# A two-layer graph network on one core: the order of work from the end of the update to the output

## The chip, the cores and the metric

The kernel runs on one core of a Trainium2 chip. The metric is the device time of one execution in microseconds (us). A core has five engines with queues of their own: TensorE (PE in the profile, with its weight loads as PEld), VectorE (DVE), ScalarE (ACT), GpSimd (POOL) and SyncE (SP), which here only issues transfers. They wait for each other through semaphores.

## The reference, cut to what matters

```python
# x [256, 1024]; W [1024, 1024]; a [1, 2048]; 8192 edges
x = layernorm(x + L0(x, src, dst, ...))          # L0: edge attention, then the update
h = x @ W
al, ar = h @ a[0, :1024], h @ a[0, 1024:]
e = exp(-leaky_relu(al[src] + ar[dst], 0.1))
rowsum = segment_sum(e, src)
h_prime = segment_sum(e[:, None] * h[dst], src) / (rowsum[:, None] + 1e-5)
x = layernorm(x + elu(h_prime))
```

L0 ends in the update: `relu([x, z] @ W_hn + b_hn)` for the first 64 rows and `relu([x, z] @ W_on + b_on)` for the other 192, where z is the attention's weighted sum.

## The kernel before, in words

**Tiling.** The 256 nodes are two halves of 128 rows (index h or m), the 1024 features 8 pieces of 128 (KC, index c). Fp32 products that need full precision are made of two rounded parts: every weight matrix is streamed in chunks of 128 rows by 1024, two chunks to a transfer of 1 MB into one of four slots of `W_raw`. `high(n)` (ScalarE, line 461) rounds chunk n into `W_hi`, `low(n)` (VectorE, line 726) subtracts that from the raw chunk into `W_lo`. Both are rings of four (NB); so `high(n)` waits until TensorE has used the chunk four before it (semaphore `chunk_used`). A few chunks (`apart`) have high parts in buffers of their own. For each chunk and half TensorE multiplies `xT_hi` by W_hi and W_lo and `xT_lo` by W_hi, into two halves of 512 columns: six matmuls.

**Order.** Everything is written out by hand: each engine's instructions run in the order of its own function, and named stages (`PE_STAGES`, `ACT_STAGES`, `DVE_STAGES`) count how far an engine is. `link` makes VectorE wait for its own instruction, `stage(name)` lets others wait for it. Chunks 48 to 79 are the update's, 80 to 87 are the second layer's W.

**Update to second layer.** TensorE runs the last four chunks of the update in two passes (`update`, lines 1393 and 1394): first the part that belongs to rows 0 to 127, then rows 128 to 255. Meanwhile ScalarE, after the casts of chunks 76 to 79, loads the table for the square root (`warm_up`, line 652), copies two quarter results from PSUM (lines 655 and 657), and VectorE merges them, adds x and makes the row sums (`merge`, lines 1022 and 1023), then the mean (`mean0`). ScalarE makes the squared deviation (line 634) and the root (line 640), VectorE the inverse (line 1034) and x1 (line 1038). TensorE transposes x1's first half, eight blocks (line 1399); ScalarE rounds it (`x1_high`, line 649), VectorE makes its lows (`x1_low`, line 1043), and TensorE starts h = x1 @ W (`h_chunk`, line 1409): chunks 80 to 83 with half 0, with the eight transposes of half 1 behind the second chunk, chunks 80 to 83 with half 1, chunks 84 to 87 with half 0 (end: stage `h_0`), then chunks 84 to 87 with half 1, first columns 0 to 511 (`h_1`), then the rest. The casts and lows of chunks 78 to 83 lie between these steps.

**Attention.** VectorE takes the two dot products of h's rows with the vector a (`dot`, line 1072: half 0 whole, half 1 in two pieces). The first product, spread on a diagonal (`source_dots`, line 1077), goes through a matmul with ones (stage `al`, then `albc`, line 1431) that gives al to every partition. VectorE adds ar (line 1098), makes the leaky relu (line 1099), ScalarE the exponential (line 675), VectorE multiplies by the number of edges (line 1103, stages `ET0`, `ET1`). ScalarE copies h to SBUF (line 672).

**Output.** TensorE makes half 0 of h_prime with eight instructions (`hp`, line 1435, stage `hp0`), then the row sums (line 1446, `sums`), then half 1. Row sums become inverses (lines 1106 to 1108). ScalarE makes the relu (line 679) and the exponential (line 683) of the elu, VectorE joins them (`elu_and_add`, lines 1115 and 1117). A second layer norm follows: deviations on ScalarE, one half after the other, each with its root; `normalise` on VectorE; half 1's last 512 columns on ScalarE (line 701). Three transfers take the result out: half 0 (line 344), then the two column halves of half 1 (lines 346 and 704). GpSimd subtracts 1 from x1 (line 447), beside it all, once x1 is transposed.

Of the kernel before, what the change touches and what calls it, by code (L numbers as in the profile page):

```python
# [5 lines left out]
P = 128  # L6
N = 256
# [32 lines left out]
def gnn_two_layers(nc, x, src, dst, W_hh, b_hh, W_oo, b_oo, W_ho, b_ho, W_a, b_a, W_hn, b_hn, W_on, b_on,  # L40
# [6 lines left out]
    with ctx:  # L47
# [50 lines left out]
        y_sums, less_mean, squares, rstd = (small[:, k:k + 4] for k in (46, 50, 54, 58))  # L98

# [140 lines left out]
        x1_less_one = sem("x1_less_one")  # L240
        squared = sem("squared")
# [42 lines left out]
        def halves(n):  # L284

            if apart(n):
                return hi_apart[n - END["hoB"] - NB], lo_in_raw[:, n // 2 % NS, n % 2, :]
            return W_hi[:, ring(n), :], W_lo[:, ring(n), :]

        def lo_count(n, pool):  # L290
# [5 lines left out]
                     "x1T0", "x1T1", "h_0", "h_1", "albc", "hp0", "sums", "hp1", "hp2"]  # L296
        ACT_STAGES = ["xT0", "xT1", "hh_x", "ooB_out", "C_hh", "C_oo", "L_oo", "L_hh", "counts", "parts", "soft0", "soft1", "zT0", "both0", "zT1",
                      "both1", "q0_low", "q1_low", "sd0", "x1T0", "sd1", "x1T1", "h1_0", "h1_1",
                      "exp0", "exp1", "h_relu0", "h_exp0", "h_exp1", "h_relu1", "h_exp2", "h_relu2", "sd2", "sd3", "out3"]
        DVE_STAGES = ["xT0", "xT1", "tot", "totals", "columns", "ooA_out", "placed0", "placed1", "keys", "key_u8", "hoA_b",  # L300
                      "hoA_lo", "hoB_lo", "maxima", "P", "PT", "parts", "zT0",
                      "zT1", "mean0", "x1_0", "mean1", "x1T0", "x1_1", "x1T1", "dots0", "al", "dots1", "lr0", "lr1", "ET0", "ET1",
                      "row_sums", "mean2", "mean3", "out0", "scale3", "out1"]
# [14 lines left out]
        def _(sp):  # L318
# [27 lines left out]
            sp.dma_start(out[P:N, 0:512], y2[:, 1, 0:512]).then_inc(out_in, 16)  # L346
# [4 lines left out]
        def _(pool):  # L351
# [93 lines left out]
            ga.nop().then_inc(pick_made, 1)  # L445
            pool.wait_ge(pe_step, pe_at("x1T1"))
# [4 lines left out]
        def _(act):  # L451
# [178 lines left out]
            highs(UX + 4, END["hn"])  # L630
# [16 lines left out]
            def x1_high(h):  # L647
                act.wait_ge(pe_step, pe_at(f"x1T{h}"))
                sa.copy(xT_hi[:, :, h * P:(h + 1) * P], G0[:, h * D:(h + 1) * D].rearrange("p (c n) -> p c n", n=P)) \
                    .then_inc(act_step, 1)  # L650

            warm_up(ACT.Sqrt, 0)

# [821 lines left out]
```

## Time and profile before

| | us |
|---|---|
| median of 3 runs | 364.58 (363.96 to 365.58) |
| the profiled execution, its own time | 364.0 |
| its span, first to last instruction | 361.9 |
| PE, DVE, ACT, POOL busy in the span | 323.3, 292.6, 195.6, 109.2 |
| mean granted TensorE clock in the span | 0.959 of full speed |

The span is what the trace covers; 2.1 us of the execution's own time lie around it. The rows come from a timeline (instructions in order of time), from groups of instructions, and from windows, which give busy times and the granted clock of a stretch. Where an engine was idle before an instruction, brackets give that time and who ended it. A matmul's printed duration overlaps the next one's.

### The profile page before, as it was taken

To read this page: it belongs to the slowest core of one execution; us is meant where nothing else is said; L and a number is where in the kernel's file an instruction comes from. 1 tells how busy PE (TensorE), PEld (TensorE's weight loads), DVE (VectorE), ACT (ScalarE), POOL (GpSimd) and SP (SyncE) were. 2 spreads that over 40 slices of the span, in tenths; PEclk is the share of its full clock that TensorE was granted. 3 is DMA by queue.
4 is the path that set the end of the run, shared out by engine and by line. 5 is a ranking of instruction groups with operands and counts; after the bars stand their busy time and mean duration, and the time that the engine had idled before them with its cause. 6 is when DMAs were issued, how large, how long until landed. Compare 5 with 4: busy or idle time off the path is not lost.

```text
span 361.9 us, 4632 instructions
## 1 busy us (share of the span) xinstructions
PE 323.3 (89%) x1440; PEld 250.2 (69%) x1440; DVE 292.6 (81%) x418; ACT 195.6 (54%) x300; POOL 109.2 (30%) x123
## 2 busy tenths in 40 slices
PE   2889999999999997999999999995899997799480
PEld 1768887677645785788888888783687875588230
DVE  0799999967699978799999999986958678745535
ACT  3754396203044236788888887454435677353255
POOL 4300061083001900188889888300000000050000
PEclk9999999999999999899999999998899999699796
DMA  6999499789999994003030000026635984000003
GB/s 229 404 406 361 173 308 388 235 279 239 325 321 309 390 366 192 2 0 118 3 116 2 1 3 0 2 63 227 232 117 201 358 283 203 0 2 1 0 0 116
DMA packets 17638, 63.10 MB, mean 174 GB/s; under 512 B 2234, under 2 KB 2236, under 8 KB 17360
## 3 DMA queue, kind: packets, MB, share of 16 engines
q1 hardware_dynamic: 13520, 50.07, 37.8%
q0 software_dynamic: 2096, 8.74, 8.3%
q10 hardware_dynamic: 2000, 4.00, 3.4%
q8 instruction: 13, 0.21, 0.2%
q14 instruction: 9, 0.07, 0.1%
HBM read 59.64 MB, written 3.16 MB: 174 GB/s over the span
## 4 chain that ended last, share of the span: by engine, by line
PE 68%; DVE 21%; ACT 5%; issue 3%; DMA 2%; SPq 0%; DVEq 0%; ACTq 0%
PE ps L1313 21%; PE ps L1160 12%; PE ps L1204 8%; PE ps L1409 7%; DVE W_lo L731 5%; PE ps L1347 5%; PE ps L1320 3%; PE ps L1355 3%; PE ps L1179 3%; DMA x_nat<-in_x_dram 2%; PE ps L1435 2%; ACT W_hi L466 1%; DVE tile_val L751 1%; PE ps L1236 1%; PE ps L1218 1%
## 5 line engine op out<-in xcount | busy, mean ns | idle before, releaser
L466 ACT CAST W_hi<-W_raw 128x1024 fp32r<-128x1024 f32 x68 | 69.3, 1046 | 62.4 <-DMA W_raw<-in_L_gnn_W_ho_dram 24.6
L731 DVE TENSOR_TENSOR W_lo<-W_raw,W_hi 128x1024 fp32r<-128x1024 f32 x64 | 76.5, 1223 | 16.6 <-ACT W_hi L466 13.8
L968 DVE SCALAR_TENSOR_TENSOR ps<-ps,wa_bc 128x1024 f32<-128x1024 f32 x74 | 87.6, 1256 | 2.8 <-PE ps L1313 2.7
L1313 PE MATMUL ps<-A_tab,oh 128*128 x148 | 53.9, 446 | 2.4 <-ACT oh L575 2.4
L1160 PE MATMUL ps<-W_hi,xT_hi 128*128 128x512 f32 x112 | 46.4, 414 | 0.7 <-DVE W_lo L731 0.7
L1313 PE MATMUL ps<-B_tab,oh 128*128 x148 | 47.0, 399 | 0.0
L1160 PE MATMUL ps<-W_lo,xT_hi 128*128 128x512 f32 x112 | 44.2, 394 | 0.0
L1160 PE MATMUL ps<-W_hi,xT_lo 128*128 128x512 f32 x112 | 34.9, 393 | 0.0
L422 POOL TENSOR_SCALAR sc<-sc 128x256 f32<-128x256 f32 x37 | 32.7, 883 | 3.3
L420 POOL TENSOR_TENSOR sc<-irow,keys 128x256 f32<-128x256 f32 x37 | 23.8, 642 | 32.4 <-PE ps L1320 32.1
L581 ACT ACTIVATE sc<-sc,keys 128x64 f32<-128x64 f32 x74 | 24.4, 341 | 16.2 <-DVE ps L968 16.1
L1313 PEld LDWEIGHTS ps<-B_tab,oh 128*128 128x128 f32 x148 | 28.4, 192 | 5.4
L1320 PEld LDWEIGHTS ps<-sc 128*128 128x128 f32 x148 | 27.3, 189 | 6.4 <-issue 0.2
L447 POOL TENSOR_SCALAR x<-x 128x2048 f32<-128x2048 f32 x1 | 5.4, 5390 | 83.8 <-PE ps L1399 83.8
L1204 PE MATMUL ps<-W_raw,hh_x 128*128 128x512 f32 x64 | 28.2, 593 | 0.0
L1313 PEld LDWEIGHTS ps<-A_tab,oh 128*128 128x128 f32 x148 | 24.3, 192 | 3.9 <-issue 3.3
L1160 PEld LDWEIGHTS ps<-W_hi,xT_hi 128*128 128x128 f32 x112 | 21.5, 192 | 6.8 <-DVE W_lo L731 1.9
L568 ACT ACTIVATE oh_dist<-key_rows,pcol 128x512 bf16<-128x512 uint8 x37 | 26.1, 706 | 0.0
L575 ACT ACTIVATE oh<-oh_dist 128x512 fp32r<-128x512 bf16 x37 | 23.2, 626 | 3.6 <-PE ps L1313 3.2
L1160 PEld LDWEIGHTS ps<-W_lo,xT_hi 128*128 128x128 f32 x112 | 21.3, 191 | 4.7 <-issue 0.7
L1160 PEld LDWEIGHTS ps<-W_hi,xT_lo 128*128 128x128 f32 x112 | 21.3, 190 | 4.7
L1320 PE MATMUL ps<-sc 128*128 128x64 f32 x148 | 24.1, 247 | 0.0
(255 smaller groups left out, 553.4 us busy)
## 6 DMA issues: line engine op xcount, KB each, us to landing
W_raw<-in_L_gnn_W_oo_dram SPq DMA_DIRECT2D x8, 1024.0 KB, 9.7
W_raw<-in_L_gnn_W_ho_dram SPq DMA_DIRECT2D x8, 1024.0 KB, 5.2
W_raw<-in_L_gnn_W_hh_dram SPq DMA_DIRECT2D x8, 1024.0 KB, 8.6
W_raw<-in_L_gnn_W_hn_dram SPq DMA_DIRECT2D x8, 1024.0 KB, 5.2
W_raw<-in_L_gnn_W_on_dram SPq DMA_DIRECT2D x8, 1024.0 KB, 4.9
W_raw<-in_L_gnn_W_dram SPq DMA_DIRECT2D x4, 1024.0 KB, 4.9
key_rows<-key_rows_scratch POOLq DMA_DIRECT2D x1, 2304.0 KB, 13.9
table_scratch<-tabs ACTq DMA_DIRECT2D x2, 1024.0 KB, 6.4
```

The costliest lines, as they stand in the source:

```text
L420: link(ga.tensor_tensor(pair, irow[:, 1:Q + 1].unsqueeze(1).unsqueeze(1).broadcast_to([P, 2, 2, Q]), keys[:, t:t + 2, 0:2].unsqueeze(3).br ...
L422: ga.tensor_scalar(pair, pair, 0.0, None, ALU.is_equal).then_inc(ends_made, 1)
L466: sa.copy(halves(n)[0], W_raw[:, n // 2 % NS, n % 2, :]).then_inc(hi_made, 1)
L568: sa.activation(oh_dist[:, j % 2, :, :], key_rows[:, :, 2 * j * P:2 * (j + 1) * P], ACT.Abs, bias=pcol[:, 1:2]).then_inc(dist_made, 1)
L581: sa.activation(sc[:, t % U, 2, :], sc[:, t % U, 1, :], ACT.Copy, scale=keys[:, t, 2:3]) \
L731: v.tensor_tensor(lo, W_raw[:, n // 2 % NS, n % 2, :], hi.bitcast(F32), ALU.subtract).then_inc(lo_made, 1)
L968: v.scalar_tensor_tensor(acc, acc, 0.0, wa_bc[:], ALU.max, ALU.mult, accum_out=keys[:, t, 2:3]).then_inc(reduced, 1)
L1160: ins = mm(acc[:, m * D + f:m * D + f + 512], x_part(n - first, m), W[:, f:f + 512], start=(n == first and x_part is hi and W is W1), stop ...
L1204: ins = mm(G0[:, f:f + 512], hh_x[:, row // KC, row % KC, :], W_raw[:, n // 2 % NS, n % 2, f:f + 512], start=(row == 0), stop=(row == 2 * ...
L1313: ins = mm(acc[:, n * 512:(n + 1) * 512], oh[:, t // 2 % 2, k, t % 2 * P:(t % 2 + 1) * P], tab[:].rearrange("p q d -> p (q d)")[:, n * 512 ...
L1320: ins = mm(G0[:, bass.ds(column.with_bounds(min_val=0, max_val=15 * Q), Q)], sc[:, t % U, 1:3, :].rearrange("p r n -> p (r n)"), sc[:, t % ...
L1409: ins = mm(G1[:, m * D + f:m * D + f + 512], part[:, c, m * P:(m + 1) * P], W[:, f:f + 512], start=(c == 0 and part is xT_hi and W is W1), ...
```

## The change

It acts on seven places, all but one behind the last casts of the update:

1. Chunks 80 and 81 get high parts in two separate buffers, and are cast by ScalarE and subtracted by VectorE before the square root's table load and the merges. The casts of the six other chunks stand one place or more earlier in the row as well. The lows of all eight overwrite the raw chunk.
2. x1's first half is normalised, transposed, rounded and given its lows in two pieces of four blocks.
3. TensorE runs chunks 80 to 85 (not 83) with half 0 and then half 1; behind these are left two chunks (not four) with half 0 (`h_0`) and with half 1.
4. GpSimd negates the second half of a (`bias_bc[:, 1, :]`, 128 by 1024) once the last biases are there; VectorE's dots then give -ar.
5. exp(-leaky_relu(s)) becomes the smaller of exp(-s) and exp(-0.1 s): ScalarE makes both from PSUM, VectorE takes the minimum and multiplies. The adding and the leaky relu on VectorE go.
6. TensorE makes the row sums of each half ahead of that half's part of h_prime; ScalarE makes the exponential ahead of the relu.
7. In the last layer norm half 0's squared deviation goes from ScalarE to VectorE, behind `mean3`; one root and one inverse serve both halves; VectorE normalises half 1 whole; half 1 goes out as two transfers of 64 rows.

```diff
+            return END["hoB"] + NB <= n < UX or END["upd"] <= n < END["upd"] + 2
...
+            if late(n):
+                return (hi_apart[2 + n - END["upd"]] if apart(n) else W_hi[:, ring(n), :]), in_place
...
-            sp.dma_start(out[P:N, 0:512], y2[:, 1, 0:512]).then_inc(out_in, 16)
+            sp.dma_start(out[P:P + Q, :], y2[0:Q, 1, :]).then_inc(out_in, 16)
...
+            pool.wait_ge(biases_in, 112)
+            ga.tensor_scalar(bias_bc[:, 1, :], bias_bc[:, 1, :], -1.0, None, ALU.mult).then_inc(less_target, 1)
...
-            highs(UX + 4, END["hn"])
+            highs(UX + 4, END["upd"] + 2 - NB)
...
             warm_up(ACT.Sqrt, 0)
             act.wait_ge(chunk_used, END["hn"])
             sa.copy(y2[0:Q, 0, :], G0[Q:P, D:2 * D]).then_inc(act_step, 1)
             act.wait_ge(pe_step, pe_at("q1"))
             sa.copy(y2[Q:P, 0, :], G1[0:Q, 0:D]).then_inc(act_step, 1)
-            highs(END["hn"], END["hn"] + 2)
+            high(END["upd"] + 2)
+            high(END["upd"] + 3)
             act.wait_ge(dve_step, dve_at("mean0"))
             deviation(0, x1[:, 0, :])
-            root(0, 1)
-            highs(END["hn"] + 2, END["upd"])
-            x1_high(0)
+            root(0, 1, 1)
+            high(END["upd"] + 4)
+            x1_high(0, 0, KC // 2, "x1T0a")
             act.wait_ge(dve_step, dve_at("mean1"))
             deviation(1, x1[:, 1, :])
-            root(1, 2)
-            x1_high(1)
-            highs(END["upd"], END["h1"])
+            root(1, 2, 2)
+            high(END["upd"] + 5)
+            x1_high(0, KC // 2, KC, "x1T0b")
+            x1_high(1, 0, KC, "x1T1")
+            high(END["upd"] + 6)
+            high(END["upd"] + 7)
...
+            def powers(h):
+                sa.activation(PT[:, h, :], G0[:, 0:N], ACT.Exp, bias=dots[:, h, 1:2], scale=-1.0)
+                sa.activation(y2[:, 1, h * N:(h + 1) * N], G0[:, 0:N], ACT.Exp, bias=slopes[:, h:h + 1], scale=-SLOPE) \
+                    .then_inc(act_step, 1)
...
+            act.wait_ge(dve_step, dve_at("dots0"))
+            h_copy(0, 0, D)
+            act.wait_ge(dve_step, dve_at("dots1a"))
+            h_copy(1, 0, 512)
+            act.wait_ge(pe_step, pe_at("albc"))
+            powers(0)
+            act.wait_ge(dve_step, dve_at("dots1"))
+            powers(1)
+            h_copy(1, 512, D)
...
-            act.wait_ge(dve_step, dve_at("mean2"))
-            deviation(0, h1[:, 0, :])
-            root(0, 3)
+            warm_up(ACT.Sqrt, 0)
             act.wait_ge(dve_step, dve_at("mean3"))
             deviation(1, h1[:, 1, :])
-            root(1, 4)
+            act.wait_ge(dve_step, dve_at("square2"))
+            root(0, 2, 3)
...
-            lows(UX + NB + 4, END["upd"])
+            lows(UX + NB + 4, END["upd"] + 2)
...
-            low(END["upd"])
-            inverse(0, "sd0")
-            normalise(x1[:, 0, :], y1[:, 0, :], 0)
-            stage("x1_0")
+            low(END["upd"] + 2)
+            inverse(0, 1, "sd0")
+            normalise(x1[:, 0, 0:512], y1[:, 0, 0:512], 0)
+            stage("x1_0a")
...
-            low(END["upd"] + 1)
-            x1_low(0)
-            inverse(1, "sd1")
+            x1_low(0, 0, KC // 2, "x1T0a")
+            low(END["upd"] + 3)
+            normalise(x1[:, 0, 512:D], y1[:, 0, 512:D], 0)
+            stage("x1_0b")
+            inverse(1, 2, "sd1")
             normalise(x1[:, 1, :], y1[:, 1, :], 1)
             stage("x1_1")
-            lows(END["upd"] + 2, END["upd"] + NB)
-            x1_low(1)
-            lows(END["upd"] + NB, END["h1"])
+            low(END["upd"] + 4)
+            x1_low(0, KC // 2, KC, "x1T0b")
+            low(END["upd"] + 5)
+            x1_low(1, 0, KC, "x1T1")
+            lows(END["upd"] + 6, END["h1"])
...
+            link(v.tensor_scalar(slopes[:, 0:1], dots[:, 0, 1:2], SLOPE, None, ALU.mult))
             stage("dots0")
...
-                link(v.tensor_scalar(PT[:, h, :], G0[:, 0:N], dots[:, h, 1:2], None, ALU.add))
-                link(v.scalar_tensor_tensor(PT[:, h, :], PT[:, h, :], SLOPE, PT[:, h, :], ALU.mult, ALU.max))
...
+                link(v.tensor_tensor(PT[:, h, :], PT[:, h, :], y2[:, 1, h * N:(h + 1) * N], ALU.min))
                 link(v.tensor_tensor(PT[:, h, :], PT[:, h, :], S_cnt[:, 0, h, :], ALU.mult))
...
-            inverse(0, "sd2")
+            link(v.scalar_tensor_tensor(h1[:, 0, :], y1[:, 0, :], less_mean[:, 0:1], y1[:, 0, :], ALU.add, ALU.mult,
+                                        accum_out=squares[:, 0:1]))
+            stage("square2")
+            inverse(0, 2, "sd2")
             normalise(y2[:, 0, :], y1[:, 0, :], 0)
             stage("out0")
...
-            normalise(y2[:, 1, 0:512], y1[:, 1, 0:512], 1)
+            normalise(y2[:, 1, :], y1[:, 1, :], 1)
...
+            both = END["upd"] + 6
+            transpose_x1(0, 0, KC // 2, "x1_0a", "x1T0a")
+            pe.wait_ge(dve_step, dve_at("x1T0a"))
+            for n in range(END["upd"], both):
+                if n == END["upd"] + KC // 2:
+                    pe.wait_ge(dve_step, dve_at("x1T0b"))
                 h_chunk(n, 0, (0, 512))
...
                 pe.wait_ge(dve_step, dve_at(f"ET{hd}"))
+                for hs in range(2):
+                    ins = mm(bank(1 + hs)[:, 0:1], PT[:, hd, hs * P:(hs + 1) * P], ones_f[:, 0:1],
+                             start=(hd == 0), stop=(hd == 1))
+                if hd == 1:
+                    stage(ins, "sums")
```

## Rows read from the trace of the kernel before

**Rows 1.** The page's chain that ended last, shares of the span by engine:

```profile
PE 68%; DVE 21%; ACT 5%; issue 3%; DMA 2%; SPq 0%; DVEq 0%; ACTq 0%
```

**Rows 2.** Timeline, end of update to restart: start us, us, engine line op [idle before <-releaser]:

```profile
293.89 2.95 ACT L466 CAST W_hi<-W_raw 128x1024 fp32r<-128x1024 f32 x3 [1.29 <-PE ps L1355]
296.85 1.28 ACT L645 ACT_TABLE_LOAD   x1
298.36 1.01 ACT L655 COPY y<-ps 64x1024 f32<-64x1024 f32 x1
...
304.72 1.15 ACT L634 ACTIVATE x<-y,small 128x1024 f32<-128x1024 f32 x1 [0.77 <-DVEq L724]
...
307.45 1.48 PE L1399 MATMUL ps<-ident,x 128*128 128x128 f32 x8 [2.12 <-DVEq L724]
...
311.52 0.79 PE L1409 MATMUL ps<-W_hi,xT_hi 128*128 128x512 f32 x1 [2.59 <-DVEq L724]
```

**Rows 3.** Timeline, the attention's dots and h_prime:

```profile
331.11 1.23 DVE L1072 SCALAR_TENSOR_TENSOR y<-ps,bias_bc 128x1024 f32<-128x1024 f32 x1 [3.50 <-PE ps L1409]
...
336.20 0.69 DVE L1072 SCALAR_TENSOR_TENSOR y<-ps,bias_bc 128x512 f32<-128x512 f32 x1 [0.69 <-PE ps L1409]
...
337.52 0.70 PE L1431 MATMUL ps<-y,ones_f 128*128 128x256 f32 x2 [1.44 <-DVEq L724]
...
341.31 5.79 PE L1435 MATMUL ps<-h,PT 128*128 128x512 f32 x8 [3.09 <-DVEq L724]
```

**Rows 4.** Timeline, row sums and the exponential behind them:

```profile
346.94 0.95 PE L1446 MATMUL ps<-ones_f,PT 128*128 128x1 f32 x8
...
348.38 1.11 ACT L683 ACTIVATE y<-ps,small 128x1024 f32<-128x1024 f32 x1 [0.21 <-DVEq L724]
```

**Rows 5.** Timeline, the last layer norm:

```profile
355.97 1.15 ACT L634 ACTIVATE h<-y,small 128x1024 f32<-128x1024 f32 x1 [0.59 <-DVEq L724]
...
358.92 0.34 ACTq L704 DMA_DIRECT2D out_dram<-y  x1
```

**Rows 6.** Windows: PE, PEld, DVE, ACT, POOL busy us, PEclk, DMA share, GB/s:

```profile
314.50:315.00 0.50, 0.50 (x3) 0.36 (x3) 0.50 (x1) 0.00 (x0) 0.00 (x0) 0.66 0.00 0
...
338.50:339.00 0.50, 0.00 (x0) 0.00 (x0) 0.41 (x1) 0.46 (x1) 0.00 (x0) 0.73 0.00 0
...
345.50:346.00 0.50, 0.50 (x2) 0.19 (x1) 0.00 (x0) 0.00 (x0) 0.00 (x0) 0.94 0.00 0
```

**Rows 7.** Timelines of POOL and its neighbours on DVE and ACT, four stretches:

```profile
118.61 0.60 POOL L435 CAST x_both<-xT_hi 128x512 fp32r<-128x512 f32 x1
118.88 0.35 DVE L867 TENSOR_TENSOR rest<-st_logit,part_f 128x1 f32<-128x1 f32 x1
...
239.53 1.91 ACT L612 CAST bn_parts<-y 64x2048 fp32r<-64x2048 f32 x1 [1.60 <-DMA y<-in_L_gnn_b_on_dram]
241.69 0.70 DVE L901 TENSOR_TENSOR S_log<-S_log,junk 128x512 f32<-128x512 f32 x1
...
317.03 5.39 POOL L447 TENSOR_SCALAR x<-x 128x2048 f32<-128x2048 f32 x1 [83.83 <-PE ps L1399]
318.03 1.23 DVE L1043 TENSOR_TENSOR xT_lo<-ps,xT_hi 128x1024 fp32r<-128x1024 f32 x1 [2.96 <-ACT xT_hi L649]
...
322.28 1.23 DVE L731 TENSOR_TENSOR W_lo<-W_raw,W_hi 128x1024 fp32r<-128x1024 f32 x1 [3.02 <-ACT W_hi L466]
```

**Rows 8.** Groups kept apart by shape, 295 to 362 us: xcount | busy us, mean ns:

```profile
L1038 DVE TENSOR_SCALAR x<-y,small 128x1024 f32<-128x1024 f32 x2 | 1.6, 813 | 0.1
...
L1103 DVE TENSOR_TENSOR PT<-PT,S_cnt 128x256 f32<-128x256 f32 x2 | 0.8, 425 | 0.3
...
L675 ACT ACTIVATE PT<-PT 128x256 f32<-128x256 f32 x2 | 0.8, 418 | 0.8 <-DVEq L724 0.7
...
L1038 DVE TENSOR_SCALAR y<-y,small 128x512 f32<-128x512 f32 x1 | 0.5, 546 | 0.1
```

**Rows 9.** Transfers, 355 to 362 us in 40 slices: GB/s moved:

```profile
GB/s 0 0 0 0 0 0 0 0 0 0 0 0 0 0 0 0 23 468 398 398 374 445 398 421 71 0 211 374 398 386 375 375 374 386 117 0 0 0 0 0
```

More of the change, by code:

```diff
@@ L635, in deviation, with root @@
                     .then_inc(squared, 1)
-            def root(h, nth):
+            def root(a, b, nth):
                 act.wait_ge(squared, nth)
-                sa.activation(deviations[:, h:h + 1], squares[:, h:h + 1], ACT.Sqrt, bias=eps_ln[:, 0:1], scale=1.0 / D) \
+                sa.activation(deviations[:, a:b], squares[:, a:b], ACT.Sqrt, bias=eps_ln[:, 0:1], scale=1.0 / D) \
                     .then_inc(act_step, 1)
@@ L1087, in _ @@
                 dot(1, k, 0, 512, dot_parts[:, 0, k:k + 1])
+            stage("dots1a")
             dve.wait_ge(chunk_used, END["h1"])
@@ L1094, in _ @@
                     stage("al")
+            link(v.tensor_scalar(slopes[:, 1:2], dots[:, 1, 1:2], SLOPE, None, ALU.mult))
             stage("dots1")
-            dve.wait_ge(pe_step, pe_at("albc"))
-            for h in range(2):
-                link(v.tensor_scalar(PT[:, h, :], G0[:, 0:N], dots[:, h, 1:2], None, ALU.add))
-                link(v.scalar_tensor_tensor(PT[:, h, :], PT[:, h, :], SLOPE, PT[:, h, :], ALU.mult, ALU.max))
-                stage(f"lr{h}")
             for h in range(2):
                 dve.wait_ge(act_step, act_at(f"exp{h}"))
+                link(v.tensor_tensor(PT[:, h, :], PT[:, h, :], y2[:, 1, h * N:(h + 1) * N], ALU.min))
                 link(v.tensor_tensor(PT[:, h, :], PT[:, h, :], S_cnt[:, 0, h, :], ALU.mult))
@@ L1394, in _, with transpose_x1 @@
             update(END["hn"], END["upd"], (1,))
-            def transpose_x1(h):
-                pe.wait_ge(dve_step, dve_at(f"x1_{h}"))
-                for c in range(KC):
+            def transpose_x1(h, a, b, ready, name):
+                pe.wait_ge(dve_step, dve_at(ready))
+                for c in range(a, b):
                     ins = nc.tensor.transpose(G0[:, h * D + c * P:h * D + (c + 1) * P], x1[:, h, c * P:(c + 1) * P],
                                               ident[:])
-                stage(ins, f"x1T{h}")
+                stage(ins, name)
             def h_chunk(n, m, columns):
@@ L1439, in _ @@
                 pe.wait_ge(dve_step, dve_at(f"ET{hd}"))
-                pe.wait_ge(act_step, act_at("h1_1"))
+                for hs in range(2):
[3 more added lines that the diff above has]
+                    stage(ins, "sums")
                 for n in range(2):
+                    if hd and n:
+                        pe.wait_ge(act_step, act_at("h1_1"))
                     ins = hp(0, n, hd)
             stage(ins, "hp0")
-            for hs in range(2):
-                for hd in range(2):
-                    ins = mm(G0[:, 512 + hs * N:512 + hs * N + 1], PT[:, hd, hs * P:(hs + 1) * P], ones_f[:, 0:1],
-                             start=(hd == 0), stop=(hd == 1))
-            stage(ins, "sums")
             for n in range(2):
```

82 lines of the change are left out of this document (38 added, 44 removed).

## The prediction

> **What bounds the kernel now.** I read the page's chain first: it lies 68% on PE and 21% on DVE [rows 1], so an edit pays where PE stands still or where the chain has left it. All of the change but one instruction acts on the last 65 us; there the timeline shows where PE stops. Behind the update it waits until 311.52, with eight transposes between at 307.45 [rows 2]; behind h it stops at about 336.1 and starts h_prime at 341.31 [rows 3]; from the row sums on, the chain is ACT and DVE alone, until the last transfer is issued at 358.92 [rows 4, 5]. The windows show a second cost of these stops: the granted clock is 1.2 GHz (0.50) when PE restarts, and is back at 2.4 GHz at about 314.8 and 345.5, 3.3 and 4.2 us after the restarts [rows 3, 6]. The groups by shape give durations.
>
> **1. GpSimd's scaling of a: +0.65.** The new instruction is not free, though POOL stands idle for 83.8 us [rows 7]. It may start when the last bias lands, at 239.5 (ACT's cast starts there). It is half as large as the 5.39 us subtraction of the same kind [rows 7]: some 2.8 us with its fixed part, so it ends at about 242.3. On DVE, L901 is due at 241.69, a TENSOR_TENSOR with both inputs in SBUF, in the unbroken chain of the softmax. Can it run beside POOL? At 118.88 a TENSOR_TENSOR with both inputs in SBUF, of one column, ran from 118.88 to 119.23, and POOL's cast from 118.61 to 119.21: an operation so small that lasts until POOL's is over has waited for it. Against this, a subtraction at 322.28 began 0.14 us before POOL's end at 322.42 and took its usual 1.23 [rows 7]; but an end that is off by 0.14 explains that. I take the wait: 242.3 - 241.7 = 0.65, ends 0 and 0.7. DVE's chain carries it to the zT stage, where PE waits.
> The Trainium skill's page "SBUF — State Buffer", section "Who interferes with whom", says that a VectorE instruction with two SBUF inputs and a GpSimd instruction that reads SBUF exclude each other, and the one issued second waits for the whole of the first. By that rule the sum holds the 0.65; by the row of 322.28 alone it would be 0.65 less. The row of 118.88 agrees with the rule.
>
> **2. From the update to PE's restart: -0.2.** ACT's last three casts end at 296.85, the table load follows at once, then L655 at 298.36 [rows 2]. That copy's data have been there since PE finished chunk 75; ACT alone makes it late. Two more casts ahead of the table load, at a third of 2.95 us each [rows 2], push L655 and all behind it (second copy, two merges, mean0) by 1.9. The squared deviation then starts at 306.6, not 304.72. What comes back: the casts of 82 and 83 fill ACT's wait for mean0. On DVE, one subtraction (1.2 us) leaves the path between x1 and its lows; the half normalisation takes 0.55 instead of 0.81 [rows 8]; four transposes instead of eight save half of 1.48 [rows 2], though DVE's sum of y1's second half (1.3 us) hides that; the half lows take 0.69 instead of 1.23, the price of 512 columns from PSUM [rows 3]. Step by step: x1's first piece is there at 309.0, four transposes end at 309.85, the half cast at 310.45, the half lows at 311.2, PE starts at 311.3. So 1.9 lost, 2.1 won. The second piece, chunk 84's lows and half 1's lows all come before PE needs them: x1T0b by 317.6 against 319.8, x1T1 by 320.8 against 322.5, chunk 86's lows by 329.0 against 330.8. PE's matmuls for h are the same number and have no new stop.
>
> **3. The dots: +2.05.** Before, 24 matmuls lie between h_0 and h's end, and DVE's dots start at 331.11 and 336.20 [rows 3]: 5.09 us. After, 12 lie between, so 2.55. DVE now needs 5.65 us from the first dot to `al` (331.11 to 337.45, just ahead of the broadcast at 337.52, less 0.69 idle; [rows 3]) and 0.2 more for the slope's multiply. Before, PE's end covered all but 1.25 of it. After: 336.20 - 2.55 + 5.85 = 339.5, against 337.45. DVE becomes the bound here, and the last pieces of h are ready first. Ends: 1.85 to 2.2.
>
> **4. Two exponentials: -0.95.** From `al` to the first matmul of h_prime it was 337.45 to 341.31, 3.86 us [rows 3]. After: the broadcast, 0.70 before [rows 3], which now comes at 339.5, behind the clock's fall at about 338.7 [rows 6], so at 1.2 GHz about 0.95 with its start; two exponentials of 0.42 [rows 8] behind it; minimum and product, 0.425 each [rows 8]; 0.3 for six handovers. Sum 2.9. The exponential's source in PSUM and the copies of h in between cost nothing: ACT has finished them by 338.6.
>
> **5. Row sums ahead, exponential ahead of relu: +0.35 and -1.25.** Before, hp0 takes 5.80 (341.31 to 347.11), and the exponential starts 1.27 later, behind relu, sums and inverse [rows 4]. After, it starts at once: -1.25, because the sums end 1.7 us before hp0. But PE makes them first: eight instructions took 0.80 at 2.4 GHz [rows 4]; four at 1.2 GHz cost 0.8 to 1.3, four at 2.4 GHz 0.4, and of the former half comes back, as less of h_prime then runs at 1.2 GHz. Together 0.6 with a restart as slow as before, 0.2 with one of 3.4 us; I take 0.35. The relu is behind the exponential but ends before DVE's first addition does.
>
> **6. The last layer norm: +1.0.** Before, mean3 releases the deviation at 355.97, and the last transfer is issued at 358.92, 2.95 us later [rows 5]. After: square on DVE 1.3 (beside ACT's), root 0.3, inverse 0.2, normalise half 0 0.81, half 1 0.81 [rows 8], handovers 0.2: 3.6. And half 0 goes out only 0.85 before half 1, not 1.8. In the slices of 0.175 us the two halves of the output moved at about 390 GB/s, with a pause between [rows 9]. After, 1 MB moves in one stretch of 2.65 us that begins some 0.85 behind the first issue (358.75 in this execution's times), and ends at 362.2 against 361.2. So +1.0, +0.65 if only the issue counts.
>
> **Sum.** 0.65 - 0.2 + 2.05 - 0.95 + 0.35 - 1.25 + 1.0 = +1.65. Some 0.1 of step 2 and 0.1 to 0.2 of step 5 depend on when the clock rises; I round to +1.5. The profiled execution took 364.0 (span 361.9), so 365.5; the median of the runs, 364.58, is 0.6 above it, so 366.1. A measurement of this kernel can't tell less than 0.5% (1.8 us) from no change; the forecast is just within it, and the ends of the steps (0 in step 1, 1.85 and 2.2 in step 3, 0.2 and 0.6 in step 5, 0.65 in step 6) give 364.8 to 367.1.
>
> **Rivals.**
> *POOL's scaling is hidden* (12%): step 1 is 0, as by the row of 322.28; 364.58 + 0.9 = 365.5.
> *The clock isn't lowered in a gap* (10%): in the gap ahead of h, PE ran 1.48 us of transposes and still restarted at 1.2 GHz [rows 2, 6]; the new gap has fewer. Against it, then; but the new broadcast at 339.5 lies in the middle of the second gap. A restart at 2.4 GHz gives back half of 3.3 to 4.2 us: about 364.2, and 362.4 if both gaps keep the clock. This one ends faster.
> *DVE's lows behind POOL* (6%), slower: POOL's subtraction of 5.39 us starts when half 1's transposes end, 318.45; DVE's `low(85)`, with both inputs in SBUF, is due at 317.6. Should it come second, it waits until 323.9, half 1's lows come at 326.4 instead of 320.8, and PE, free at 322.5, waits 3.9 us: 370.0. It decides when DVE is more than 0.85 us later than drawn. The lows themselves, one input in PSUM, do run beside POOL: 1.23 at 318.03 [rows 7].
> *A slower restart* (10%), slower: the dots leave PE idle for 3.4 us before the broadcast and 1.7 behind it. If the clock stays at 1.2 GHz through the first half of h_prime, step 5 costs 2 more: 368.
> *The change doesn't do what it says*: x1 by pieces is meant to bring PE's restart forward, and the two early casts take all of that back. That is in the forecast, as step 2.
>
> **How the numbers follow.** Forecast 62%, the rivals 12, 10, 6 and 10%. Slower by over 0.5% means above 366.4: about two fifths of the forecast's case, and both slow rivals: 0.42. Faster by over 0.5% (below 362.8) needs the clock in both gaps: 0.06. The rest, 0.52, is within. The range goes from the one gap with a clock kept to the slower restart: 364.0 to 368.0; it leaves out the double clock case and the wait behind POOL.
>
> **What would show it.** Step 1: L901's place (the TENSOR_TENSOR behind the reciprocal) takes 1.3 instead of 0.70. Step 2: the first copy of the quarters starts 1.9 later behind the last cast of chunk 79, PE's restart lies within 0.3 of 6.2 us behind the update's end. Step 3: no idle time on DVE between the dots, `al` 3.4 us behind PE's last matmul of h instead of 1.3. Step 4: 2.9 us from there to h_prime. Step 5: row sums long ready, an exponential at once behind hp0. Step 6: 3.6 us from mean3 to the last issue, one stretch of transfers. Wrong would be: DVE idle between the dots, a stop of PE among h's matmuls, or a restart at the full clock.

## The result, and the profile of the changed kernel

The changed kernel takes 370.13 us (median of 4 runs, 369.62 to 371.23), the kernel before 364.73 beside it: a ratio of 1.0166, 95% interval 1.0136 to 1.0196. A second series, below, gave 369.16 and a ratio of 1.0127 (1.0098 to 1.0156). The forecast was 366.1, 1.5 us above the kernel before, with a range from 364.0 to 368.0: the direction was right, the size less than a third of the true one (5.4 us, and 5.0 in the second series). The runs of the kernel before fall in two groups, and its one trace is of the second: of 17 runs beside experiments 1 to 4, 7 took 362.9 to 363.3 at a mean granted clock of 0.963, and 10 took 364.1 to 365.5 at 0.959.

| | before | changed, first trace | changed, second trace | forecast |
|---|---|---|---|---|
| update's end | 305.33 | 307.90 | 305.61 | +0.65 |
| from there to h's first matmul | 6.19 | 6.30 | 6.30 | -0.2 |
| h | 24.56 | 25.37 | 25.48 | 0 |
| h's end to the broadcast of al | 1.44 | 3.46 | 3.46 | +2.05 |
| to h_prime's first instruction | 3.79 | 3.13 | 3.13 | -0.95 |
| to the elu's exponential | 7.07 | 7.71 | 7.73 | -0.9 |
| to the last deviation | 7.59 | 7.59 | 7.59 | 0 |
| to the last transfer's issue | 2.95 | 3.85 | 3.84 | +0.65 |
| to the span's end | 2.96 | 4.18 | 4.19 | +0.35 |
| span | 361.88 | 369.49 | 367.33 | +1.65 |

The table is worked out from starts and ends in the timelines (us); the line for the update's end is a time in the span, the others are lengths. The columns before and second trace differ by 5.45 in all: 0.28 + 0.11 + 0.92 + 2.02 - 0.66 + 0.66 + 0.89 + 1.23. The first trace holds 2.3 us more ahead of the update's end than the second. The 0.28 at the update's end is not shown to be the change's: in the traces of experiments 2 to 6 and 9 to 11, which differ by one instruction at most up to there, the update's end lies between 304.15 and 306.27.

The timeline of the changed kernel (first trace) around the update's end, 307.90:

```profile
299.30 1.99 ACT L477 CAST hi<-W_raw 128x1024 fp32r<-128x1024 f32 x2
301.31 1.28 ACT L655 ACT_TABLE_LOAD   x1
302.82 1.01 ACT L664 COPY y<-ps 64x1024 f32<-64x1024 f32 x1
...
311.63 1.12 PE L1426 MATMUL ps<-ident,x 128*128 128x128 f32 x4 [3.72 <-DVEq L747]
...
314.20 0.80 PE L1436 MATMUL ps<-hi,xT_hi 128*128 128x512 f32 x1 [1.46 <-DVEq L747]
```

The two early casts stand ahead of the table load. Against [rows 2] the transposes have shrunk from 1.48 to 1.12 and the second wait of PE from 2.59 to 1.46, but the first has grown from 2.12 to 3.72.

From the dots to the exponential, the same trace:

```profile
341.70 0.69 DVE L1100 SCALAR_TENSOR_TENSOR y<-ps,bias_bc 128x512 f32<-128x512 f32 x1
...
343.03 1.22 PE L1463 MATMUL ps<-y,ones_f 128*128 128x256 f32 x2 [3.46 <-DVEq L747]
...
346.16 1.01 PE L1473 MATMUL ps<-ones_f,PT 128*128 128x1 f32 x4 [1.91 <-DVEq L747]
347.03 3.76 PE L1467 MATMUL ps<-h,PT 128*128 128x512 f32 x4
...
353.87 1.11 ACT L710 ACTIVATE y<-ps,small 128x1024 f32<-128x1024 f32 x1 [7.54 <-PE ps L1467]
```

The third pair of dots carries no bracket: DVE no longer waits for PE, as it did by 0.69 in [rows 3], and PE waits 3.46 for the broadcast's operand. The granted clock of that stretch (windows; columns as in [rows 6]):

```profile
345.00:348.00 3.00, 1.84 (x5) 1.35 (x6) 1.70 (x4) 1.34 (x4) 0.00 (x0) 0.50 0.00 0
348.00:351.00 3.00, 3.00 (x7) 1.42 (x5) 0.00 (x0) 0.00 (x0) 0.00 (x0) 0.50 0.00 0
351.00:354.00 3.00, 3.00 (x8) 1.63 (x8) 0.32 (x2) 0.13 (x1) 0.00 (x0) 0.76 0.00 0
```

0.76 of the last 3 us is a rise at about 352.4, 6.3 us behind h_prime's start; in the kernel before it came 4.2 us behind [rows 3, 6].

The end, timeline and transfer issues (KB each, us from issue to landing):

```profile
361.46 1.15 ACT L645 ACTIVATE h<-y,small 128x1024 f32<-128x1024 f32 x1 [1.47 <-DVEq L747]
361.53 1.28 DVE L1154 SCALAR_TENSOR_TENSOR h<-y,small 128x1024 f32<-128x1024 f32 x1 [0.16 <-DVE small L1051]
...
365.31 0.55 ACTq L727 DMA_DIRECT2D out_dram<-y  x1
```

```profile
out_dram<-y SPq DMA_DIRECT2D x1, 512.0 KB, 2.6
out_dram<-y SPq DMA_DIRECT2D x1, 256.0 KB, 3.1
out_dram<-y ACTq DMA_DIRECT2D x1, 256.0 KB, 3.8
```

In the kernel before, the last transfer was issued 2.95 us behind the deviation [rows 5], here 3.85; and the last landing takes 3.8 us.

### The profile page after: what moved, and what is told of

It is laid out like the page before. It is cut to its first block, busy times and chain, and to the rows that moved or that the text cites. A ratio compares the mean times of both kernels' runs of the same rounds, so it can differ in the third digit from the quotient of the medians.

```text
span 369.5 us, 4635 instructions
## 1 busy us (share of the span) xinstructions
PE 327.0 (88%) x1440; PEld 252.6 (68%) x1440; DVE 293.6 (79%) x420; ACT 194.5 (53%) x301; POOL 110.9 (30%) x124
## 4 chain that ended last, share of the span: by engine, by line
PE 69%; DVE 20%; ACT 5%; issue 2%; DMA 2%; SPq 0%; DVEq 0%; ACTq 0%
PE ps L1340 21%; PE ps L1187 11%; PE ps L1231 7%; PE ps L1436 6%; DVE W_lo L754 5%; PE ps L1374 5%; PE ps L1347 3%; PE ps L1382 3%; PE ps L1206 3%; PE ps L1467 3%; DMA x_nat<-in_x_dram 2%; PE ps L1406 1%; ACT W_hi L477 1%; DVE tile_val L774 1%; DVE y L1100 1%
## 5 line engine op out<-in xcount | busy, mean ns | idle before, releaser
L477 ACT CAST W_hi<-W_raw 128x1024 fp32r<-128x1024 f32 x66 | 67.2, 1045 | 65.0 <-DMA W_raw<-in_L_gnn_W_ho_dram 24.7
L754 DVE TENSOR_TENSOR W_lo<-W_raw,W_hi 128x1024 fp32r<-128x1024 f32 x56 | 66.8, 1222 | 13.3 <-ACT W_hi L477 11.2
```

The source lines that it names most:

```text
L477: sa.copy(halves(n)[0], W_raw[:, n // 2 % NS, n % 2, :]).then_inc(hi_made, 1)
L754: v.tensor_tensor(lo, W_raw[:, n // 2 % NS, n % 2, :], hi.bitcast(F32), ALU.subtract).then_inc(lo_made, 1)
```

## The experiments

Each was run beside the kernel before on the same chip, whose medians were 364.11 to 364.19. A difference "by the ratios" is the difference of two ratios to the kernel before, times 364. The theory at first: my steps hold, and what is missing in the sum is time at 1.2 GHz. The rival: work that I did not count.

### 1. and 2. Both kernels with PE kept busy in its gaps

```diff
+            def fill(b, count):
+                for _ in range(count):
+                    mm(bank(b), zT_hi[:, 0, 0:P], flat(zT_hi, 0, 2), start=True, stop=True, skip_group_check=True)
...
+            fill(0, 8)                       # changed kernel: 14
             transpose_x1(0)
+            fill(3, 10)                      # changed kernel: 6
             pe.wait_ge(dve_step, dve_at("x1T0"))
...
+            fill(3, 5)                       # changed kernel: 13
             pe.wait_ge(dve_step, dve_at("al"))
             stage(mm(G0[:, 0:N], ones_f[:], y2[:, 0, 0:N], start=True, stop=True), "albc")
+            fill(3, 12)                      # changed kernel: 9
```

> The kernel before with 35 matmuls whose results nobody reads, on PE where it stands idle: 8 ahead of x1's first transposes, 10 behind them, 5 ahead of the broadcast of al, 12 behind it, each some 0.23 us at 2.4 GHz. Clock theory: PE restarts at the full clock in both places, which gives back half of the 3.3 us before h's clock rises and half of the 4.2 us in h_prime, so 1.5 to 3.7 us less than before. Rival (the clock costs nothing, other engines set the end): within 0.5 us of before.

Measured: 360.29 us, ratio 0.9901 (0.9882 to 0.9920): 3.9 us faster, just past the expected 3.7. The clock stays at 2.4 GHz from the update to h_prime's end.

> The changed kernel with 42 such matmuls in its own gaps: 14 ahead of the first transposes, 6 behind, 13 ahead of the broadcast, 9 behind. Clock theory: what the change lost beyond the 1.5 us of my sum (5.4 measured) is longer time at 1.2 GHz (10.2 us at a stretch in h_prime's trace instead of 6.8, and later in h), so this kernel is 3 to 5 us faster than the changed one, and 1 to 2 us slower than the kernel before with such matmuls. Rival (work I did not count on ACT, DVE or in transfers): it stays 4 us or more behind the kernel before with such matmuls.

Measured: 363.92 us, ratio 1.0004 (0.9986 to 1.0022), so by the ratios 4.5 us faster than the changed kernel's second series and 5.9 faster than its first. But it is 3.6 us slower than the kernel before with such matmuls, where I expected 1 to 2. Both theories are half right. At the same full clock the two timelines differ as follows: h 23.49 against 22.99; h's end to broadcast 3.46 against 1.44; to h_prime 2.63 against 3.80; to the exponential 4.60 against 4.97; to the last issue (from the last deviation) 3.85 against 2.95; from there to the end 4.19 against 2.96. What the sum did not count is in three places: 0.5 in h, 0.5 of the 0.9 promised by step 5, and 1.1 in the last layer norm and transfers (2.1 against the forecast's 1.0). The way from h_prime's start to the exponential, in this trace:

```profile
341.36 0.58 PE L1481 MATMUL ps<-ones_f,PT 128*128 128x1 f32 x4
341.80 1.96 PE L1475 MATMUL ps<-h,PT 128*128 128x512 f32 x4
...
345.96 1.11 ACT L710 ACTIVATE y<-ps,small 128x1024 f32<-128x1024 f32 x1 [4.45 <-PE ps L1475]
```

### 3. Four chunks left behind h's first part

```diff
-            both = END["upd"] + 6
+            both = END["upd"] + 4
```

> The changed kernel, with chunks 80 to 83 (not 85) through both halves first, so four chunks are left behind them as before: only step 3 undone. My theory: the dots start 2.55 us earlier against h's end, DVE is not the bound, al comes 2.05 us earlier, and h_prime starts that much earlier: 2 us less than the changed kernel, up to 3.5 if the clock has not fallen so far. Rival (the order of chunks is free, the dots lie elsewhere hidden): within 0.5 us of the changed kernel.

Measured: 366.66 us, ratio 1.0067 (1.0043 to 1.0091): 2.2 us less by the ratios against the second series of the changed kernel, 3.6 against the first. VectorE waits again, and h's end to broadcast is 1.36:

```profile
338.72 0.69 DVE L1100 SCALAR_TENSOR_TENSOR y<-ps,bias_bc 128x512 f32<-128x512 f32 x1 [0.77 <-PE ps L1436]
```

Step 3 stands: its row returns with one edit. But that the total came out as expected is partly luck, as two more terms stand in this trace, of opposite sign. PE stops in h, because four chunks with half 0 end ahead of half 1's lows, which are done at 321.92:

```profile
322.03 0.50 PE L1436 MATMUL ps<-hi,xT_hi 128*128 128x512 f32 x1 [1.05 <-DVEq L747]
```

so h takes 26.73 us against 25.48: the two chunks more of step 3 do buy something, which my sum put at nothing. And the clock is back sooner in h_prime, which starts at 342.66:

```profile
343.00:343.50 0.50, 0.50 (x4) 0.40 (x4) 0.47 (x2) 0.00 (x0) 0.00 (x0) 0.96 0.00 0
343.50:344.00 0.50, 0.50 (x2) 0.19 (x1) 0.08 (x1) 0.00 (x0) 0.00 (x0) 0.50 0.00 0
...
346.00:346.50 0.50, 0.50 (x3) 0.13 (x1) 0.00 (x0) 0.00 (x0) 0.00 (x0) 0.50 0.00 0
346.50:347.00 0.50, 0.50 (x6) 0.50 (x4) 0.00 (x0) 0.00 (x0) 0.00 (x0) 0.62 0.00 0
```

The stretch at 1.2 GHz lasts 3.4 us here, against 6.8 in the kernel before and 10.2 in the changed one, and ends 4.2 us behind h_prime's start. From the broadcast to h_prime it is 2.61 instead of 3.13, and from there to the exponential 6.32 instead of 7.73. Against experiment 9 the rows are +1.25, -2.10, -0.52 and -1.41.

### 4. The old layer norm and transfers

The edit puts back the two deviations with a root each on ScalarE, `scale3`, and the transfers by columns, as the kernel before has them.

```diff
-            warm_up(ACT.Sqrt, 0)
+            act.wait_ge(dve_step, dve_at("mean2"))
+            deviation(0, h1[:, 0, :])
+            root(0, 1, 3)
             act.wait_ge(dve_step, dve_at("mean3"))
             deviation(1, h1[:, 1, :])
-            act.wait_ge(dve_step, dve_at("square2"))
-            root(0, 2, 3)
+            root(1, 2, 4)
...
-            link(v.scalar_tensor_tensor(h1[:, 0, :], y1[:, 0, :], less_mean[:, 0:1], y1[:, 0, :], ALU.add, ALU.mult,
-                                        accum_out=squares[:, 0:1]))
...
```

> The changed kernel with the last layer norm and the three transfers of the kernel before: only step 6 undone. My theory: from mean3 to the last issue 2.95 us again instead of 3.85, and the transfers apart again: 1 to 2 us less than the changed kernel. Rival (the transfers end at the same time anyway, as their rate bounds them): less than 0.5 us less.

Measured: 366.89 us, ratio 1.0091 (1.0065 to 1.0117). From the last deviation to the span's end it is 5.90 us, as before (5.91), against 8.03 in the changed kernel. So the part costs 2.1, not 1.0. In time it is 1.3 us less than the second series of the changed kernel by the ratios, 2.3 by the medians; with runs from 365.06 to 367.95 the time alone would not tell, and the trace does.

### 5. Row sums behind, relu first

```diff
-                for hs in range(2):
-                    ins = mm(bank(1 + hs)[:, 0:1], PT[:, hd, hs * P:(hs + 1) * P], ones_f[:, 0:1], ...)
...
             stage(ins, "hp0")
+            for hs in range(2):
+                for hd in range(2):
+                    ins = mm(bank(1 + hs)[:, 0:1], PT[:, hd, hs * P:(hs + 1) * P], ones_f[:, 0:1], ...)
+            stage(ins, "sums")
```

> The changed kernel with the row sums made behind hp0 and the relu ahead of the exponential, as before: only step 6's neighbour, step 5, undone. By my sum this costs 1.25 and returns 0.35: 0.9 us slower than the changed kernel. Clock theory: in the changed kernel's trace h_prime began with four of the one-column matmuls at 346.16 and the clock rose only at 352.4, 6.2 us later, against 4.2 in the kernel before; if the small matmuls at the head delay the rise, this kernel's clock is back up to 3.4 us sooner, which gives back up to 1.7: between 0.8 faster and 0.9 slower than the changed kernel, and from the first hp matmul to hp0's end 5.8 us again. From al to h_prime nothing changes.

Measured: 369.26 us, ratio 1.0125 (1.0089 to 1.0162), the same as the changed kernel within the noise. The timeline:

```profile
343.61 6.58 PE L1467 MATMUL ps<-h,PT 128*128 128x512 f32 x8 [1.91 <-DVEq L747]
350.03 0.95 PE L1479 MATMUL ps<-ones_f,PT 128*128 128x1 f32 x8
```

The eight instructions take 6.5 us instead of the 5.80 of [rows 3, 4], without a small matmul at their head, and the clock is back at 349.5, 5.8 us behind the start (0.55 in the window 349.0 to 349.5, 1.00 in the next). So my idea that the small matmuls delay the clock falls. The way from h_prime's start to the exponential is 7.86 here and 7.73 with the sums ahead: at this clock step 5 by itself is worth 0.13.

### 6. Without GpSimd's scaling

```diff
-            ga.tensor_scalar(bias_bc[:, 1, :], bias_bc[:, 1, :], -1.0, None, ALU.mult).then_inc(less_target, 1)
+            ga.nop().then_inc(less_target, 1)
```

> The changed kernel without GpSimd's scaling of a's second half: it leaves out the negation, so the exponentials get al minus instead of plus the bias; all else is the same work. My step 1 said the scaling costs 0.65 by making a subtraction on VectorE wait. The changed kernel's trace already speaks against it: VectorE's L924 began at 243.05 and took 0.69 while POOL ran from 240.98 to 243.77. So by step 1: 0.65 less than the changed kernel; by that trace: within 0.3.

Measured: 368.90 us, ratio 1.0119 (1.0075 to 1.0163); the changed kernel's second series had 1.0127. From the first copy of the logits on DVE to the zT lows it is 23.81 us with the scaling (trace of experiment 5) and without it. The rows of the changed kernel (first trace) show why:

```profile
240.98 2.79 POOL L456 TENSOR_SCALAR bias_bc<-bias_bc 128x1024 f32<-128x1024 f32 x1 [6.44 <-DMA y<-in_L_gnn_b_on_dram]
```

```profile
243.05 0.69 DVE L924 TENSOR_TENSOR S_log<-S_log,junk 128x512 f32<-128x512 f32 x1
```

The subtraction (VectorE's TENSOR_TENSOR) starts 0.72 us ahead of POOL's end, as far as the trace places that end, and takes its usual time. Step 1 was nothing.

### 7. The casts of 80 and 81 late

```diff
-            highs(UX + 4, END["upd"] + 2 - NB)
+            highs(UX + 4, END["upd"] - NB)
...
             sa.copy(y2[Q:P, 0, :], G1[0:Q, 0:D]).then_inc(act_step, 1)
+            high(END["upd"])
+            high(END["upd"] + 1)
             high(END["upd"] + 2)
```

with VectorE's `low(80)` to `low(84)` one place or more later, between x1's steps. The edit also moves GpSimd's subtraction from x1 behind the last lows, so the two are tested together.

> The changed kernel with the casts and lows of chunks 80 and 81 behind the quarter copies and merges (ScalarE casts 80 to 83 there, VectorE's lows are spread between x1's steps), and GpSimd's subtraction from x1 behind the last lows. Theory of step 2: the first quarter copy starts 1.5 us behind chunk 79's cast again instead of 3.4, mean0 comes 1.9 earlier, and PE's restart some 2 us earlier than in the changed kernel against the update's end (4.2 instead of 6.3). The end follows by 2, give or take 1.7 for the clock. Rival (the early casts are needed, PE then waits for the lows of 80 to 83): PE stops between h's first chunks and less than 0.7 us comes out.

Measured: 366.98 us, ratio 1.0083 (1.0054 to 1.0112): 1.6 us less than the second series by the ratios, 3.0 than the first.

```profile
297.49 1.28 ACT L656 ACT_TABLE_LOAD   x1
299.00 1.01 ACT L665 COPY y<-ps 64x1024 f32<-64x1024 f32 x1
```

```profile
307.82 0.65 PE L1431 MATMUL ps<-ident,x 128*128 128x128 f32 x4 [1.83 <-DVEq L750]
310.22 0.74 PE L1441 MATMUL ps<-hi,xT_hi 128*128 128x512 f32 x1 [1.75 <-DVEq L750]
```

PE restarts 4.23 us behind the update's end (305.99), against 6.30 with early casts and 6.19 before; GpSimd's subtraction starts only at 329.71, far behind it. Step 2's bookkeeping is shown: the pieces win 2 us at the restart, the early casts lose as much.

### 8. What should be kept, with filled gaps

The changed kernel with the edits of 3, 4 and 7, the lows of 84 and 85 behind half 1's, and unread matmuls in the four gaps:

```diff
+            fill(0, 7)
             transpose_x1(0, 0, KC // 2, "x1_0a", "x1T0a")
+            fill(3, 7)
...
+            fill(3, 5)
             pe.wait_ge(dve_step, dve_at("al"))
             stage(mm(G0[:, 0:N], ones_f[:], y2[:, 0, 0:N], start=True, stop=True), "albc")
+            fill(3, 8)
```

> What the steps say should be kept: of the change the two pieces of x1, the lows in place, the two exponentials and the row sums ahead; casts of 80 and 81 late, four chunks left behind h's first part, the last layer norm of before, and 27 unread matmuls that keep PE busy in its gaps. By the steps, against the kernel before with such matmuls (360.29): restart -1.5 (2 won, 0.45 for the four transposes moved behind it), exponentials -1.1, row sums and order -0.4: 357.3, some 7 us less than before. Rival (the pieces only pay where PE is bound, and the lows now come too late at the full clock): 359 to 360.

Measured: 358.64 us, ratio 0.9869 (0.9831 to 0.9907; four runs took 358.28 to 358.64, two 360.86 and 360.89): 1.3 us above the expectation, but the fastest median of this study, 5.5 us below the kernel before (4.8 by the ratio). The timeline of PE shows a wait of 1.04 in h, which is most of the missing part:

```profile
316.12 0.61 PE L1447 MATMUL ps<-W_hi,xT_lo 128*128 128x512 f32 x2
317.79 0.50 PE L1447 MATMUL ps<-hi,xT_hi 128*128 128x512 f32 x1 [1.04 <-DVEq L754]
```

h's first four chunks are done before half 1's lows, as in experiment 3. Against experiment 1 PE restarts 1.94 us earlier (4.23 against 6.17), but h takes 1.82 longer (24.81 against 22.99): of the win of x1's pieces 0.1 is left at the full clock, much as the rival says. What is left of the gain on experiment 1 is 1.2 ahead of h_prime and 0.33 behind its start.

### 9. The changed kernel again

> The changed kernel once more, unchanged. Its first trace had two stretches at 1.2 GHz in code that the change does not touch (3.4 us more at 148, and 263.7 to 267.1 in the second z product), which put the update's end at 307.9, while the traces of four variants have it at 304.2 to 306.0. Theory: that was this execution, not the change; the update ends at 305.3 to 306.3 here and the median lies 5 us above the kernel before, of which 4.65 is the sum of the steps as the variants' traces show them. Rival: the change itself moves that stretch; then the update ends at 307 to 308 again.

Measured: 369.16 us, ratio 1.0127 (1.0098 to 1.0156). The update ends at 305.61. The 2.3 us that the first trace had ahead of it belong to that execution. The other rows agree with the first trace within 0.11 us.

### 10. The last transfers by columns

```diff
-            sp.dma_start(out[P:P + Q, :], y2[0:Q, 1, :]).then_inc(out_in, 16)
+            sp.dma_start(out[P:N, 0:512], y2[:, 1, 0:512]).then_inc(out_in, 16)
...
-            act.dma_start(out[P + Q:N, :], y2[Q:P, 1, :]).then_inc(out_in, 16)
+            act.dma_start(out[P:N, 512:D], y2[:, 1, 512:D]).then_inc(out_in, 16)
```

> The changed kernel with half 1 going out as two transfers of 128 rows by 512 columns (as before) instead of 64 rows by 1024; the last layer norm stays changed. In the changed kernel's trace these took 3.1 and 3.8 us from issue to landing, and 2.0 and 2.6 in the kernel before; from the last issue to the span's end it was 4.2 against 3.0. Theory A (the form of 64 rows): 2.0 to 2.9 again and 0.8 to 1.2 us less at the end. Theory B (they stand behind half 0's 512 KB, issued 1 us before): 3 us or more still, and less than 0.4 us less.

Measured: 368.33 us, ratio 1.0116 (1.0081 to 1.0150); that it is faster than the changed kernel is inside the intervals, so the trace has to tell. Its issues:

```profile
out_dram<-y SPq DMA_DIRECT2D x1, 512.0 KB, 2.7
out_dram<-y SPq DMA_DIRECT2D x1, 256.0 KB, 2.8
out_dram<-y ACTq DMA_DIRECT2D x1, 256.0 KB, 3.1
```

From the last issue to the end it is 3.46 us, against 4.19 with rows and 2.96 before. Of the 1.2 us, 0.7 are the form of 64 rows (theory A). The other 0.5 go with the new layer norm (with the old one, experiment 4, it is 2.95); that they are spent behind half 0's transfer (theory B) fits, but was not tried by itself.

### 11. Only the gap ahead of h_prime filled

The edit of experiment 2 without its first two fills; against that kernel:

```diff
-            fill(0, 14)
...
-            fill(3, 6)
```

> The changed kernel with unread matmuls only in the second gap, 13 ahead of the broadcast of al and 9 behind it. Clock theory: from h_prime's first instruction to the elu's exponential it is 4.6 us (as in the kernel with both gaps filled) instead of 7.6; the broadcast takes 0.70 instead of 1.22; all of 3.4 us is won on the changed kernel, against 1.4 for this gap in the kernel before, where the clock rose 4.2 us behind h_prime's start and not 6. Rival (row sums ahead make the stretch long by themselves): over 5.5 us.

Measured: 365.58 us, ratio 1.0028 (1.0010 to 1.0045): 3.6 us less than experiment 9 in the same series.

```profile
340.78 0.70 PE L1470 MATMUL ps<-y,ones_f 128*128 128x256 f32 x2 [0.46 <-DVEq L747]
...
343.40 0.59 PE L1481 MATMUL ps<-ones_f,PT 128*128 128x1 f32 x4
...
345.66 0.50 PE L1481 MATMUL ps<-ones_f,PT 128*128 128x1 f32 x4
```

```profile
348.02 1.11 ACT L710 ACTIVATE y<-ps,small 128x1024 f32<-128x1024 f32 x1 [4.46 <-PE ps L1475]
```

From h_prime's start to the exponential 4.62 us, against 7.73: in the changed kernel 3.1 us of this stage are the clock. In the kernel before it is 7.07 - 4.97 = 2.1 (experiment 1). That 1.0 is the change's own loss to the clock here.

### 12. Five chunks first, and a gap in the softmax filled

Experiment 8 with one chunk more ahead of half 1, 15 unread matmuls ahead of P's transposes, and one unread matmul more in two of the four gaps; against experiment 8:

```diff
+            low(END["upd"] + 4)
             x1_low(1, 0, KC, "x1T1")
-            lows(END["upd"] + 4, END["h1"])
+            lows(END["upd"] + 5, END["h1"])
...
+            pe.wait_ge(dve_step, dve_at("maxima"))
+            for _ in range(15):
+                mm(bank(1), xT_hi[:, 0, 0:P], flat(xT_hi, 0, 2), start=True, stop=True, skip_group_check=True)
...
-            both = END["upd"] + 4
+            both = END["upd"] + 5
```

> The kernel with late casts, old layer norm and filled gaps (358.64), now with five chunks through both halves first, and the lows of chunk 84 ahead of half 1's, because there PE stopped for 1.2 us (316.6 to 317.8) waiting for half 1's lows; also 15 unread matmuls ahead of the transposes of P. The stop goes but for 0.3, al comes 0.4 later against h's end, the transposes run at 2.4 GHz (0.4): 357.4 to 358. Rival (the stop is taken over by the lows of 84 and 85): 358.6 as before.

Measured: 360.59 us, ratio 0.9887 (0.9850 to 0.9923): slower than expected by 3. The stretch at 1.2 GHz that lay at 250.6 to 257.4 in experiment 8 has moved to 260.4 to 267.3, and now covers the second z product: the update ends at 307.65, not 305.39. The only edit ahead of that place is the 15 unread matmuls, but the first trace of the changed kernel and that of experiment 10 have part of this stretch there without them, so one trace does not settle the cause; one of the six runs took 357.24. Behind the update's end, h is 24.15 instead of 24.81, but h's end to broadcast is 2.10 instead of 1.37: five chunks win nothing on four.

## Why the forecast was wrong

The stages of the two kernels differ by 5.45 in all in the traces; the forecast's sum was 1.65, rounded to 1.5. The step that failed most is step 5: it took 0.9 off where the traces add 0.66, because it let the clock come back in h_prime as soon as before. Beside it, the matmuls of h were put at nothing (0.92) and the last transfers too low (1.23 instead of 0.35). Point by point:

**Step 1 (+0.65) was wrong: 0.** VectorE's subtraction ran beside POOL's scaling (experiment 6). The row of 322.28 in [rows 7], which I explained away with an inexact end, was the one to go by. The wait at 118.88 was real in its row, but it does not carry over to this pair of instructions; what the two cases differ in was not tried. The trace of the kernel before does show the two engines excluding each other elsewhere: GpSimd's TENSOR_SCALAR of line 422 at 119.89 took 1.97 us beside a low of VectorE that began at 119.85 and took 1.23, against 0.88 on average. It may be that GpSimd's work is over some time before its printed end; that is not shown. The rule of the Trainium skill's page "SBUF — State Buffer", section "Who interferes with whom", makes the second instruction wait for the whole of the first; here it did not.

**Step 2 (-0.2): +0.1 at the restart, and 0.5 forgotten.** The two opposed terms are shown by experiment 7 (2.1 us between early and late casts). The forecast's -0.2 against +0.11: the four transposes ran at 1.2 GHz and took 1.12, not 0.75 (0.65 in experiment 7, at 2.4 GHz), which is as much as the miss. The sentence that failed is "PE's matmuls for h are the same number": four of half 0's transposes have moved behind the restart, and PE makes them among h's matmuls. They cost 0.5 (h at full clock 23.49 against 22.99). The rest of the 0.92 in h is the clock, back 4.3 us behind the restart in the second trace instead of 3.3: one microsecond more at half speed.

**Step 3 (+2.05): right for its row, 2.02.** Undone alone it comes back (experiment 3). What the step left out is that the longer gap goes with a later clock, below, and that the two chunks cover a stop of 1.05 us in h.

**Step 4 (-0.95): right in kind, -0.66.** With the clock up it is -1.17 (2.63 against 3.80). At 1.2 GHz the broadcast takes 1.22 instead of 0.70; I had put 0.95 for it.

**Step 5 (-0.9): the wrong sign, +0.66.** It has two errors. The sums' eight instructions all lie ahead of hp0's end now, and hp0 with them takes as much longer as they last, 0.8 at full clock (0.44 and 0.36 between the starts in experiment 2); with them the whole step is -0.37 (4.60 against 4.97). I had allowed 0.35 for them and let a half come back. And I took the clock's return as 3.4 to 4.2 us behind h_prime's start; it came 5.8 to 6.4 us behind it in seven traces (the changed kernel twice, experiments 4 to 7 and 10). That costs the 1.0 of experiment 11. In these seven h_prime starts 6.6 us behind h's end, and the stretch at 1.2 GHz lasts 10.2; in the kernel before it starts 5.2 behind, and the stretch lasts 6.8; in experiment 3, with step 5 in place and four chunks left, 4.0 and 3.4. So it isn't step 5's edit that brings the slow restart; it goes when step 3 alone is undone, and with it the longer gap. The rival "a slower restart" described this, with the dots' gap as its ground, and priced it at 2; it was given 10%.

**Step 6 (+1.0): right in kind, 2.1.** From the deviation to the last issue it is 0.9, not 0.65. The transfers cost 1.2, not 0.35: I had taken the rate of [rows 9] for any transfer; 64 rows by 1024 move slower than 128 rows by 512 (0.7 of it, experiment 10).

In sum, measured less forecast: -0.37 at the update's end, +0.31 at the restart, +0.92 in h, -0.03 in the dots, +0.29 ahead of h_prime, +1.56 in step 5, +0.24 and +0.88 in step 6: together 3.80, which with the forecast's 1.65 gives the 5.45. The upper end of the forecast's own case, 367.1, doesn't follow from the ends of its steps either: with 0.7, 2.2 and 0.6 they give 366.6. Its range to 368.0 held one slower restart and no miss in any other step.

**Rivals.** "VectorE's lows behind POOL", whose 370.0 is the measured median, is not what happened: `low(85)` began at 321.06, 0.86 ahead of POOL at 321.92, half 1's lows followed at 322.92, and PE had no stop in h. That 370.0 is the measured median is chance. "The clock isn't lowered in a gap" did not occur by itself; made by hand it is worth 3.9 us in the kernel before.

## What to carry to other kernels

An idle time of some microseconds on TensorE was paid twice here, by the gap and by the slow restart. Before an edit makes such a gap longer, ask what the restart behind it costs, and consider unread matmuls to keep the clock (3.9 us here, for 35 of them). When part of a stage is brought forward, what is left of it goes somewhere: list every instruction that now stands behind the restart. A total that comes out as expected does not prove its terms: experiment 3 met its 2 us with a stop that I had not forecast and a clock that was back sooner. Cast work placed ahead of a copy that waits only for its own engine delays the whole chain by the cast's length, however idle the engine looks later.

## What the runs showed of the hardware that I had not expected

- The clock's return behind a restart is no constant: 3.3 to 4.3 us in h, 4.2 to 6.4 in h_prime. It is not set by the one-column matmuls at the head (experiment 5). With the same instructions in h_prime it was 6.3 us behind a gap of 6.6 from h's end and 4.2 behind one of 4.0 (experiments 9 and 3); as the clock also fell at another place there, what sets it stays open.
- A stretch at 1.2 GHz can move onto work where it costs more: in experiment 12 it came 10 us later than in experiment 8, and the update's end came 2.3 us later. That the filled gap ahead of it is the cause was not shown.
- A GpSimd scaling of 128 by 1024 (2.79 us) and a VectorE subtraction with two operands in SBUF overlapped by 0.7 us in the trace without loss to the latter. Elsewhere, at 119.89 in the kernel before, a GpSimd TENSOR_SCALAR of 128 by 256 took 1.97 us instead of 0.88 beside such a subtraction that had begun 0.04 us earlier.
- Two transfers of 256 KB took 3.1 and 3.8 us as 64 rows of 4 KB, and 2.8 and 3.1 as 128 rows of 2 KB, behind the same 512 KB.
